# V projection and output products moved beside the attention of a fused cross-attention block

## The reference

```
x  = layer_norm(hidden, ln1_w, ln1_b)
q  = x @ q_w + q_b ;  k = ctx @ k_w + k_b ;  v = ctx @ v_w + v_b
attn = softmax(where(mask, q k^T / sqrt(32), min))
hidden = (attn v) @ cproj_w + cproj_b + residual
y  = layer_norm(hidden, ln2_w, ln2_b)
out = hidden + gelu(y @ fc_w + fc_b) @ proj_w + proj_b
```

## Time and profile before

| | |
|---|---|
| median of 3 runs | 822.11 us (820.63 to 826.83) |
| profiled execution, its own time | 823.19 us |
| span of that execution | 821.4 us |
| TensorE clock granted, mean | 0.992 |
| busy: PE, DVE, ACT, POOL | 788.1, 449.1, 276.6, 314.6 us |
| projections end, attention begins | 156.8 us, 158.2 us |
| MLP begins | 448.3 us |

### The profile page before, as it was taken

The page is one execution under the profiler, slowest core; times in us unless marked ns, Lnnn a source line. Parts: engine busy times, 40 slices in busy tenths (PEclk is TensorE's granted clock), DMA queues, the critical chain, the costliest instruction groups (busy, mean ns, idle before and its releaser), DMA issues.

```text
span 821.4 us, 9736 instructions
## 1 busy us (share of the span) xinstructions
PE 788.1 (96%) x3728; PEld 558.1 (68%) x3728; DVE 449.1 (55%) x711; ACT 276.6 (34%) x483; POOL 314.6 (38%) x190
## 2 busy tenths in 40 slices
PE   7899999999999998999898899999999999999998
PEld 5788888644445444544543688888888888888886
DVE  6853344787866897688789735633323332332122
ACT  4434241366654654467347101121112111111111
POOL 2724040166973875488648436432002110112000
PEclk9999999999999999999999999999999999999999
DMA  8476385836534533537331245004000400020001
GB/s 308 129 243 231 120 253 143 257 79 161 125 91 131 166 79 91 168 79 182 102 103 39 69 150 162 31 0 155 1 0 1 154 1 0 1 84 20 0 1 51
DMA packets 53102, 85.39 MB, mean 104 GB/s; under 512 B 5344, under 2 KB 13796, under 8 KB 53056
## 3 DMA queue, kind: packets, MB, share of 16 engines
q1 hardware_dynamic: 52912, 84.75, 34.8%
q10 hardware_dynamic: 144, 0.02, 0.0%
HBM read 59.45 MB, written 25.18 MB: 103 GB/s over the span
## 4 chain that ended last, share of the span: by engine, by line
PE 79%; DVE 14%; DMA 2%; issue 2%; ACT 1%; SPq 1%; POOL 0%; DVEq 0%; POOLq 0%
PE ps L383 20%; PE ps L384 20%; PE ps L385 20%; DVE mx L859 5%; PE ps L483 5%; PE ps L499 5%; PE ps L468 5%; PE ps L514 3%; DVE BIG L899 2%; DVE R L976 1%; PE ps L527 1%; DVE R L864 1%; DVE R L818 1%; DMA R<-in_k_w 1%; PE ps L442 1%
## 5 line engine op out<-in xcount | busy, mean ns | idle before, releaser
L1123 POOL TENSOR_TENSOR R<-Pt 128x1024 f32<-128x1024 f32 x59 | 144.1, 2460 | 127.3 <-PE ps L514 76.6
L859 DVE TENSOR_REDUCE mx<-ps 128x1 f32<-128x512 f32 x256 | 162.8, 680 | 40.7 <-PE ps L468 40.4
L692 ACT ACTIVATE Pt<-ps 128x512 f32<-128x512 f32 x256 | 135.0, 600 | 99.7 <-PE ps L483 96.5
L1012 DVE CAST HR<-R 128x512 fp32r<-128x512 f32 x52 | 24.2, 466 | 184.6 <-ACT R L726 184.6
L726 ACT ACTIVATE R<-ps,cols 128x512 f32<-128x512 f32 x52 | 35.9, 690 | 205.4 <-PE ps L385 205.4
L468 PE MATMUL ps<-BIG 97*128 97x512 f32 x256 | 94.6, 414 | 9.2 <-DVE mx L859 9.2
L483 PE MATMUL ps<-BIG 98*128 98x512 f32 x256 | 99.5, 433 | 3.6 <-ACT Pt L692 2.3
L483 PEld LDWEIGHTS ps<-BIG 98*128 98x128 f32 x256 | 43.9, 191 | 71.2 <-ACT Pt L692 36.8
L383 PE MATMUL ps<-BIG,HR 128*128 128x512 f32 x192 | 74.9, 390 | 2.7 <-DVE HR L1014 2.7
L383 PE MATMUL ps<-YT,BIG 128*128 128x512 f32 x192 | 75.8, 395 | 0.0
L385 PE MATMUL ps<-YT,BIG 128*128 128x512 f32 x192 | 74.8, 390 | 0.0
(11 more groups left out here) (107 smaller groups left out, 1298.0 us busy)
## 6 DMA issues: line engine op xcount, KB each, us to landing
BIG<-qs SPq DMA_DIRECT2D x48, 256.0 KB
BIG<-ks SPq DMA_DIRECT2D x48, 256.0 KB
ks<-BIG SPq DMA_DIRECT2D x32, 256.0 KB, 2.0
qs<-BIG SPq DMA_DIRECT2D x32, 256.0 KB, 5.5
R<-hd SPq DMA_DIRECT2D x28, 256.0 KB, 4.2
R<-in_x SPq DMA_DIRECT2D x16, 256.0 KB, 4.5
hd<-R SPq DMA_DIRECT2D x16, 256.0 KB, 2.0
RW<-in_fc_w SPq DMA_DIRECT2D x16, 256.0 KB, 2.8
```

The costliest lines, as they stand in the source:

```text
L692: eng.activation(Pt[:, r, j % 2, :], bank(3 + place % 3), ACT.Exp, scale=SCALE).then_inc(S["a_ra"], 1)
L859: eng.tensor_reduce(mx[:, s % 2, 4 * j + qc:4 * j + qc + 1], bank(place % 3), AX.X, ALU.max).then_inc(S["v_rb"], 1)
L1123: eng.tensor_tensor(R0[:, 2 * hp:2 * hp + 2, :], Pt[:, (r - 2) % 6, :, :], Pt[:, r, :, :], ALU.add).then_inc(S["g_ac"], 1)
```

## The change

V of batch 0 is projected as before. V of batches 1 to 3 and the output products of batches 0 to 2 become 24 "units" in attention steps, given by `BESIDE`. Each is issued as four threes of matmuls spread over its step, all in bank 5; ring a has banks 3 and 4 until step 58. `pv` stands behind the first `s1`, and both `sums` behind the third. `V` holds two batches; the space freed holds the context of the next batch, loaded a second time (`CF`) and split again (`CV`) by ACT and POOL. The 24 early `s1` of batch 3 stand three behind each of its 8 products. `y_turn`, the statistics of layer norm 2, the loads of x and `split_out` of a batch's first group move to other steps.

```diff
+        with nc.sbuf_tensor("V", [128, 2, 4, 512], F32) as V:
+            with nc.sbuf_tensor("CF", [128, 2, 4, 512], F32) as CF:
+            with nc.sbuf_tensor("CV", [128, 2, 4, 512], R) as CV:
...
+        BESIDE = {}
+        for b in range(3):
+            for c in range(4):
+                BESIDE[16 * b + (2, 10, 11, 12)[c]] = ("v", b + 1, c)
+                BESIDE[16 * (b + 1) + (4, 6, 8, 9)[c]] = ("c", b, c)
+        YT_STEPS = (43, 45, 47, 49)
...
+            def ring_a(key, late):
+                put(key, (3, 4, 5)[len(a) % 3] if late else 3 + len(a) % 2, ("a_ra", len(a) + 1))
...
+            for i in range(NI):
+                late = i >= 58
+                if i in BESIDE:
+                    put(BESIDE[i], 5, left(BESIDE[i]))
...
@@ SP @@
+            def load_context(b):
+                if b > 1:
+                    sp.wait_ge(*ready(("v", b - 1, 3)))
+                for k in range(4):
+                    eng.dma_start(CF[:, 1, k, :], cv[b][:, k, :]).then_inc(S[f"d_cv{k}"], 16)
...
                 if b == 3:
                     load_stack(1)
+                    load_context(1)
...
+                if i in (13, 29):
+                    load_context(b + 2)
...
@@ PE @@
+            def product(u, k):
+                kind, b, c = u
+                outp = psum(u) if k == 0 else bank(PSUM[u][0])
+                if kind == "v":
+                    pe.wait_ge("g_cv", 4 * b + k - 3)
+                    ins = mm3(outp, [CV[:, h, k, cols_c] for h in range(2)], [w[:, k, :] for w in WV], k == 0, k == 3)
+                else:
+                    pe.wait_ge("v_wc", k + 1)
+                    pe.wait_ge("a_ah", 4 * b + k + 1)
+                    pe.wait_ge("g_al", 4 * b + k + 1)
+                    ins = mm3(outp, [a[:, k, cols_c] for a in AT], [w[:, k, :] for w in WC], k == 0, k == 3)
...
@@ PE @@
             for i in range(NI):
                 s2(i, 0)
                 s2(i, 1)
+                if u:
+                    product(u, 0)
                 for m in range(4):
-                    if m >= 2:
-                        s2(i, m)
+                    if m in (1, 2):
+                        s2(i, m + 1)
+                    if m == 3 and i in YT_STEPS:
+                        y_turn(0, k, psum(("yt", k))).then_inc(S["p_rb"], 1)
                     if tile is not None:
                         s1(tile)
                     if turn is not None:
                         turn_maxima(turn)
-                    if m == 2 and kc == 1 and i >= 5:
-                        sums(s - 1, 3)
-                    if m == 2 and i >= 20 and 5 <= i % 16 < 9:
-                        cproj(b - 1, i % 16 - 5, bk).then_inc(S["p_rb"], 1)
-                if kc == 3:
-                    sums(s, 1)
-                if i >= 1:
-                    pv(i - 1)
+                    if m == 0 and i:
+                        pv(i - 1)
+                    if m == 2:
+                        if kc == 3:
+                            sums(s, 1)
+                        if kc == 1 and s:
+                            sums(s - 1, 3)
+                    if u and m < 3:
+                        product(u, m + 1)
...
@@ ACT, at the end of the step @@
+            def copy_v(u):
+                act.wait_ge(*ready(u))
+                eng.activation(V[:, b % 2, c, :], bank(PSUM[u][0]), ACT.Copy).then_inc(S["a_v"], 1)
+            def context_high(b, k):
+                act.wait_ge(f"d_cv{k}", 16 * b)
+                eng.activation(CV[:, 0, k, :], CF[:, 1, k, :], ACT.Copy).then_inc(S["a_cv"], 1)
...
@@ ACT, between projections and attention @@
+            for k in range(4):
+                context_high(1, k)
...
                 exp(i, 1)
+                if kc == 0 and s:
+                    copy_pv(s - 1)
...
-                if i >= 5 and kc == 0 and (s - 2) % 4 == 0:
+                if i >= 5 and kc == 2 and (s - 2) % 4 == 0:
                     split_out(s - 2)
+                if i in BESIDE and BESIDE[i][0] == "v":
+                    copy_v(BESIDE[i])
+                if i in (14, 15, 30, 31):
+                    for k in (0, 1) if i % 2 == 0 else (2, 3):
+                        context_high(i // 16 + 2, k)
...
@@ DVE, behind each K and Q product @@
                     if b == 3:
-                        maximum(8 + 2 * g)
-                        maximum(9 + 2 * g)
+                        for n in range(3):
+                            maximum(3 * g + n)
...
                     if tile is not None:
                         maximum(tile)
+                    if m == 3 and i in BESIDE and BESIDE[i][0] == "c":
+                        residual(BESIDE[i])
...
-                if 26 <= i < 30:
-                    statistics(HN, 0, 4, i - 26)
-                if 31 <= i < 39 and i % 2:
-                    norm(HN, 0, 4, (i - 31) // 2)
+                if 30 <= i < 34:
+                    statistics(HN, 0, 4, i - 30)
+                if i in (36, 38, 40, 42):
+                    norm(HN, 0, 4, (i - 36) // 2)
...
@@ POOL @@
+                if i in (15, 31):
+                    context_low(b + 2, 0)
+                    context_low(b + 2, 1)
+                if i in (16, 32):
+                    context_low(b + 1, 2)
+                    context_low(b + 1, 3)
```

More of the change, by code:

```diff
@@ L183, in cross_attention_block @@
+            return place, a, b
+        PSUM, RA, RB = plan_psum()
         NA, NB = len(RA), len(RB)
@@ L687, in exp @@
                 if i < 3:
[L688 removed]
+                    act.wait_ge(*made(3, 11))
                 else:
@@ L738, in _ @@
             for b in range(B):
-                for c in range(4):
-                    act.wait_ge("p_pj", 12 * b + c + 1)
-                    eng.activation(V[:, 4 * b + c, :], bank(proj_bank(12 * b + c)), ACT.Copy).then_inc(S["a_v"], 1)
+                for c in range(4 if b == 0 else 0):
+                    act.wait_ge(*made(0, c))
+                    eng.activation(V[:, 0, c, :], bank(PSUM[(0, c)][0]), ACT.Copy).then_inc(S["a_v"], 1)
                 for g in range(4):
@@ L928, in _ @@
             for b in range(B):
-                if b == 3:
-                    for tile in range(8):
-                        maximum(tile)
                 if 0 < b < 3:
@@ L948, in _ @@
                     if b == 3:
-                        maximum(16 + 2 * g)
-                        maximum(17 + 2 * g)
+                        for n in range(3):
+                            maximum(12 + 3 * g + n)
             for i in range(NI):
@@ L1109, in _ @@
                 x_low(b)
+            for k in range(4):
+                context_low(1, k)
             for i in range(NI):
```

300 lines of the change are left out of this document (142 added, 158 removed).

## The result

The changed kernel takes 854.8 us in the median of four runs (853.4 to 857.0), against 824.5 for the kernel before in the same session; the ratio is 1.037, with a 95% interval from 1.032 to 1.043. That is slower, and 17.8 us above the upper end of the range. The profiled execution took 853.4 us, its span is 851.6.

What follows compares the result with a forecast made beforehand. PE, busy for 96% of the span, was taken as the bound. From the profiled 823.2 us, -32.5 + 37.4 - 3.1 + 0.4 = +2.2 gave 825.4, written as 825, with a range of 813 to 837.

Steps and rivals of the forecast that it cites:

- part 3: Attention steps 4 to 51: base 189.5, units 51.7 and bank 5 waits 9.9 give 251.1 against 213.7, +37.4 us.
- price without cover: POOL's 12 low parts cost nothing; without cover each would cost its 1.3 us, 10 us for the eight inside.
- The plain group: Four plain attention steps: DVE wait of 0.59 goes, switches add 0.3, bank waits 0.29 and 0.27; 15.26 against 15.34 us.
- the late `exp`: divide_c comes later, split_out holds the next exp: steps 16, 32 and 48 lose 1.5, 2.1 and 1.0, together 4.6 us.
- Bank 5: In adjoining unit steps PE waits for residual (1.1 us) or copy_v (1.7 us) to release the bank; 9.9 us together.
- The start: Up to step 4's first exp: V leaves the projections, attention's start costs about 0; 141.7 instead of 174.16, -32.5 us.
- Steps 52 to 57: End of attention, last output products in 52, 54, 56, 57 between slab splits: 36.8 against 39.87 us, -3.1.
- Steps 58 to 63 and the MLP: Last attention steps: no s1 any more, one more switch, +0.4 us on 16.15; the MLP untouched.
- A: Bank 5 is free in time and PE fills its gaps: 814.4 us; chance 0.20.
- B: Two score banks bind in every step; some 35 further steps lose 0.27 each, 9.5 us: 835; chance 0.22.
- C: The context for V comes late, PE waits for g_cv in steps 10, 18 or 26: 833 us; chance 0.08.

Runs made afterwards that it cites:

- the edits to the start: Changed kernel, context_low behind the additions, bank 5 out first, plus tile 15 behind batch 3's first Q product and context_high behind Q products' high parts: 828.8 us.

## Why the prediction was wrong

**What failed.** The forecast was 825, the time 854.8. The step that failed is the sentence on POOL at the end of part 3: "each pair of additions is still done 3 us before `sums` and 1 before `exp` need it. Nothing." It asked only whether POOL would be late for those who wait on it, not whom POOL keeps out while it works. The "price without cover" of 1.3 us for each low part was wrong in kind as well: two low parts cost 7 us where `divide_c` stood beside them, and little elsewhere (step 17 grew by 1.5 with all four in step 16). With them moved the kernel took 839.0, so this step is 15.8 of the 29.8 us by which the median lies above the forecast. The rows of before had the sign: a norm of HN takes 2010 ns, beside POOL, and the same operation on R takes 0.53 to 0.55 us in that trace where POOL is idle. The prediction used the 2.0 as that operation's own length.

The Trainium skill has a rule that bears on it, which the prediction did not weigh: page SBUF — State Buffer, section "SBUF: two separate sides" says that DVE and GpSimd share one pair of ports under an exclusive lock, and that of a GpSimd operation and a DVE operation with two SBUF inputs the one that starts first keeps the pair for the whole instruction. By that rule `divide_c` would have been held for one operation of POOL, and the trace agrees in many places (1.80 and 1.27 above). In steps 15 and 31 it was held for four, and for five with the additions to x ahead (8.89 us), which the rule does not give; the measurement decides.

**The rest**, stretch by stretch. Steps 4 to 51 take 257.5 in the profile with `context_low` moved, 6.4 above the forecast:

- The plain group, steps 4 to 7: 15.26 forecast, 15.93 measured there. Forecast were -0.59 for DVE's maximum, +0.3 for the sums and +0.56 for the two banks, from 15.34 with its three waits of 0.1. The 0.59 did go: no `s1` of kc = 3 waits there now. Of the 0.69 that the group is above the forecast in the changed kernel (15.95), 0.42 is the held low part of `cproj_w` in step 4, the failed step once more. The other 0.27 are in PE's own blocks, 0.14 in kc = 0 and 1, 0.11 in kc = 2 and 0.03 in kc = 3. The bank waits are there, an `s2` being 0.26 late at the end of step 8 and about 0.2 at the end of step 6, where 0.29 and 0.27 were put.
- Steps 12 to 15 and 28 to 31: 2.0 and 2.6 above. The pair of `context_high` at the end of step 14 goes with 0.6 us more in that step, and steps 15 and 31 take 5.5 and 6.1. Part of it is the late `exp` that I had put into the groups behind (1.5 and 2.1), which are 1.3 and 0.6 below their forecast.
- Steps 20 to 23 and 36 to 39: 0.7 above each. In their first step stands the wait of 0.95 for `out_low`. The other groups are within 0.9 of their sums.
- Bank 5: 9.9 forecast as 1.7 three times, 1.1 four times and 0.1 three times; the rows have 1.26 and 0.92 at just these places, 7.5 us in steps 4 to 51, and taking the bank out sooner gave 8.3 in the time. Right in mechanism and place, about a third too large in size. The Trainium skill's rule that was weighed there (page Perfetto Trace Analysis, section Optimizing Tensor Performance) agrees with these rows. The prediction's 9.2 us for all of before's bank waits was a misreading: PE also waited 4.3 us for maxima ahead of output products and 2.3 for `exp`.
- The start: -32.5 forecast, -30.1 measured. The wait for the turned maxima was 1.47 where 1.6 was put; that `context_high` hides behind c_w was not contradicted. Left out were 0.7 us for the maxima's transfer, which I had said would be early. In the other kernels with this start the stretch came out at 143.9 to 146.3, and with the edits to the start at 143.0 to 145.1, so it varies by some two us from one profile to another.
- Steps 52 to 57: 36.8 and 36.4, right.
- Steps 58 to 63 and the MLP: +1.0 and +3.0. `split_out(12)` at step 58 makes `divide_c(13)` wait 3.2 us for POOL's `out_low`, DVE reaches the MLP later, and its first product waits 3.8 us instead of 2.3 for `HR`. "The MLP is untouched" was true of its code only.

**The rivals.** A (the bank free in time) is out: the waits were there. B (two score banks) was no larger in a plain group than the forecast's own 0.29 and 0.27, where 9.5 us over all steps were put on top. Outside such groups the timeline has an `s2` 0.37 late in seven steps (10, 18, 23, 26, 34, 39, 42) and about 0.48 late in steps 46 and 50, 3.5 us together; how much of that the banks are was not taken apart. C did not occur: no row shows PE waiting for the context. None of the three had what decided.

## What to carry to other kernels

Before an operation is put on POOL or moved there, look which of DVE's operations with SBUF operands run at that time and who waits for them: a free slot in POOL's own list says nothing about that. Where DVE has an operation on the critical path, give POOL a wait or other work there, and place bulk work of POOL beside DVE operations that read PSUM, as in steps 16 and 32 here. A DVE record far above its usual length, ending just behind a POOL record, is the sign to look for. Where one kind of work uses one bank alone, take it out ahead of the other work in the releasing engine's list; here two such moves gave back 8.3 us. And when one block is moved, look what it now stands ahead of: a `sums` ahead of the last `s2` made a load late for a step that no one had touched.

## What the runs showed that I had not expected

- A DVE operation of 0.67 us took 5.87 to 8.89 us beside POOL and ended 0.5 to 0.6 us after POOL's run of ready operations ended. In the changed kernel it ended at the first boundary in step 47 and at the last one in steps 15 and 31; 0.46 us in the time of a PE block decided it in step 47. The condition stays open.
- The same hold, 1.35 us long, stood in step 4 of the changed kernel, on another operation with two operands in SBUF.
- Maxima, which read PSUM, and `bn_stats` beside the same operations of POOL kept their 0.65 to 0.69 us in the kernel before.
- After the waits of 8 us PE worked at a lower clock: 0.80 and 0.82 over steps 15 and 31, 0.96 over steps 4 to 51 against 0.99 with `context_low` moved.
- Moving `sums` cost 2.9 us in the kernel before (822.4 to 825.3), with 3.1 us of waits for a load that came later, and nothing in the changed one, where the load is not behind `sums`.
